# A post-norm attention and feed-forward layer: output a step later, another order on VectorE, projection ahead of x's turn

## The chip, the cores and the metric

One core of one Trainium2 chip runs the whole layer in one launch. The metric is the device time of an execution in microseconds (us). The three runs of the kernel before took 2051.58, 2055.7 and 2059.28 us, a median of 2055.7 us.

## What is computed

The input x has 8 sequences of 1024 tokens with 256 features, all f32. The layer is attention with ternary weights and then a feed-forward part with blockwise FP4 values, each followed by a residual sum and a layer norm:

```
x = _layernorm(x + attention(x))            # 16 heads of 16
gate = fp4_linear(x, w_gate)                # 256 -> 704
y = fp4_linear(x, w_up)
h = jax.nn.silu(gate) * y
x = _layernorm(x + fp4_linear(h, w_down))   # 704 -> 256
```

fp4_linear rounds both of its inputs in blocks of 16 to the grid 0, 0.5, 1, 1.5, 2, 3, 4, 6 times a scale of the block (its largest magnitude / 6), and multiplies in f32.

## The kernel before

Every engine has one program, and semaphores order them. `project` makes q, k and v, `attend` the attention, and `feed` the rest: output projection, first norm, FP4 rounding of x, gate and up, silu, FP4 rounding of h, down product, second norm, output. Only `feed` is changed. Its work is cut into 64 tiles of 128 tokens and runs as a software pipeline that is written out step by step: in step i each engine works on tile i - lag, and the order of its stages within the step is the order of the code. The first steps lie within the attention; from about 1470 us on nothing else runs.

The stages, with their engine, lag and lines in the kernel before:

- TensorE, in this order: x1_by_width (lag 3), x's turn by a product with the identity (L1354), which waits for xq of GpSimd and for the first copies of hT of ScalarE, since both share a bank of PSUM; output_projection (lag 1, L1286); down (lag 6, L1337, and L1345 for the last 64 rows of two tiles together, in every second step); gate_and_up (lag 3, L1298: 18 products); h_by_width (lag 5, h's turn, L1309).
- ScalarE: copy_xqT (L1446); output (lag 8: the shift L1375 and L1376, then L1384 into fin); bend_x (L1416, L1420); bend_h (L1426, L1430); silu (L1399); copy_hT (L1407, L1408, L1411); x1_normal (lag 1: L1375, L1376, L1392).
- VectorE: block maxima of h and x (L1482); xqT's low part (L1517); scales (L1466), reciprocals (L1472), divisions of x and h (L1488); y, the residual sum that reads the projection in PSUM (L1537); statistics of y (L1541, L1548); the add of xm (L1495, 256 columns) and the difference xg (L1552); z, the second residual sum (L1557); the add of hm (L1495, 704 columns); statistics of z (L1563, L1573); h (L1568), which reads up in PSUM.
- GpSimd: in the last ten tiles raw and xb (L1589, L1591); rstd of the first norm (L1579, L1580); xq (L1601); hg (L1608) and hq (L1613); rstd of the second norm (L1579, L1580 again).
- SyncE issues the loads of pairs of tiles and the store of a tile (L1259, lag 8).

The names `mv` and `rstd` hold mean, variance and the inverse deviation of the two norms, one column each; `z` and `fin` have two buffers by the tile's number, `x1` has seven. A wait `due(engine, name, t.lin(1, c))` asks that the stage that signals `name` has been done for tile t and c - 1 tiles more.

## Time and profile before

| | |
|---|---|
| median of 3 runs | 2055.7 us (2051.58 to 2059.28) |
| profiled execution | 2051.83 us, span 2050.0 us |
| TensorE busy | 1987.0 us, 97% |
| VectorE busy | 1881.0 us, 92% |
| ScalarE busy | 1674.6 us, 82% |
| GpSimd busy | 751.6 us, 37% |
| granted TensorE clock, mean | 0.997 |

The profile is of one execution. PE is TensorE, PEld its weight loads, DVE VectorE, ACT ScalarE, POOL GpSimd, SPq the queue of SyncE. In a table of stretches a stretch has its busy time and its number of instructions for each engine. In a timeline an instruction stands with start, length, engine, line, operation, output and inputs; in brackets is how long its engine had been idle before it, and what ended that. In the waits, a row says who waited for whom: us in total, how often, the longest.

### The profile page before, as it was taken

What the parts mean: (1) busy time and instruction counts of PE and PEld (TensorE: products, weight loads), DVE (VectorE), ACT (ScalarE), POOL (GpSimd) and SP (SyncE); (2) the same over time, 40 slices, a digit from 0 to 9 for tenths busy, and PEclk for the clock granted to TensorE, in tenths of its full rate; (3) what the DMA queues carried; (4) which work ended last, traced back from release to release, by engine and by line L of the source; (5) the groups of instructions that cost most, each with busy time, mean ns of one, the idle gap of its engine ahead of it and who ended that gap; (6) DMA issues with size and microseconds to landing.
All of it is one profiled execution on the core that took longest, in us unless ns stands there. A gap on an engine that the chain in (4) does not pass through costs nothing.

```text
span 2050.0 us, 42089 instructions
## 1 busy us (share of the span) xinstructions
PE 1987.0 (97%) x15806; PEld 1044.0 (51%) x15806; DVE 1881.0 (92%) x2345; ACT 1674.6 (82%) x3244; POOL 751.6 (37%) x749
## 2 busy tenths in 40 slices
PE   8999999999999999999999999999999999999997
PEld 7766333333333333333333333334477777777775
DVE  4788999999999999999999999997399999999996
ACT  6656888888888888888889888888877777777775
POOL 3000446665764561100010010000155555555784
PEclk9999999999999999999999999999999999999999
DMA  7885632444354354435435444542111111111210
GB/s 234 273 248 200 110 51 45 79 96 91 75 100 93 78 95 90 90 82 103 89 71 101 91 84 88 97 91 75 43 40 47 47 40 42 47 47 52 62 32 21
DMA packets 119000, 181.40 MB, mean 88 GB/s; under 512 B 29644, under 2 KB 74444, under 8 KB 118796
## 3 DMA queue, kind: packets, MB, share of 16 engines
q1 hardware_dynamic: 111116, 171.10, 36.2%
q10 hardware_dynamic: 7392, 7.34, 1.1%
q8 instruction: 125, 2.05, 0.5%
q14 instruction: 79, 0.65, 0.1%
q0 software_dynamic: 288, 0.27, 0.1%
HBM read 103.68 MB, written 73.40 MB: 86 GB/s over the span
## 4 chain that ended last, share of the span: by engine, by line
PE 68%; POOL 13%; issue 7%; ACT 7%; DVE 4%; DMA 1%; POOLq 0%; SPq 0%; DVEq 0%
PE ps L913 29%; PE ps L966 28%; POOL hq L1613 4%; PE ps L494 4%; POOL hg L1608 4%; POOL rstd L1580 3%; PE ps L504 3%; ACT craw L1033 2%; PE ps L935 2%; POOL fq L1601 2%; POOL rstd L1579 1%; ACT xm L1420 1%; ACT bend_of_x L1416 1%; PE ps L481 1%; ACT centre L1376 1%
## 5 line engine op out<-in xcount | busy, mean ns | idle before, releaser
L1079 DVE TENSOR_REDUCE negmax<-ps 128x1 f32<-128x1024 f32 x980 | 1182.5, 1219 | 19.7 <-PE ps L913 14.1
L1025 ACT ACTIVATE room<-ps 128x512 f32<-128x512 f32 x2048 | 1102.8, 599 | 118.3 <-PE ps L935 86.7
L935 PE MATMUL ps<-qs,ks 50*128 50x512 f32 x2048 | 745.6, 449 | 1.9 <-ACT room L1025 1.0
L913 PE MATMUL ps<-ks,qs 48*128 48x512 f32 x1960 | 714.5, 444 | 0.0
L966 PE MATMUL ps<-room,vals 128*17 128x256 f32 x8192 | 637.3, 385 | 8.9 <-ACT craw L1033 0.2
L913 PEld LDWEIGHTS ps<-ks,qs 48*128 48x128 f32 x1960 | 288.6, 184 | 414.3 <-DVE negmax L1079 333.0
L164 POOL CAST mrow<-turned_rows 128x32 fp32r<-128x32 f32 x32 | 6.7, 210 | 904.3 <-DVE turned_rows L159 690.8
L966 PEld LDWEIGHTS ps<-room,vals 128*17 128x17 f32 x8192 | 140.0, 95 | 371.4 <-issue 209.5
L935 PEld LDWEIGHTS ps<-qs,ks 50*128 50x128 f32 x2048 | 304.2, 184 | 18.2 <-ACT room L1025 14.3
L1298 PE MATMUL ps<-wguT,xqT 128*128 128x512 f32 (+1 forms) x1152 | 266.8, 384 | 1.4 <-DVE xqT L1517 1.4
L1298 PEld LDWEIGHTS ps<-wguT,xqT 128*128 128x128 f32 x1152 | 210.8, 188 | 48.9 <-issue 9.6
L1337 PE MATMUL ps<-wdT,hT 128*128 128x256 f32 x640 | 150.6, 382 | 5.0 <-ACT hT L1408 5.0
L1136 POOL TENSOR_SCALAR fq<-fq 88x1024 f32<-88x1024 f32 (+1 forms) x42 | 137.5, 3274 | 3.6
L1375 ACT ACTIVATE centre<-mv 128x1 f32<-128x1 f32 x128 | 25.5, 199 | 132.5 <-POOL rstd L1580 132.3
L1337 PEld LDWEIGHTS ps<-wdT,hT 128*128 128x128 f32 x640 | 122.1, 192 | 22.8 <-issue 5.6
L1608 POOL TENSOR_TENSOR hg<-room,hm 128x704 f32<-128x704 f32 x64 | 97.7, 1526 | 45.7 <-DVE room L1495 45.7
L1579 POOL TENSOR_TENSOR rstd<-mv,numbers 128x1 f32<-128x1 f32 x128 | 33.9, 265 | 202.1 <-DVE mv L1548 195.2
L1495 DVE TENSOR_TENSOR room<-room,hm 128x704 f32<-128x704 f32 x64 | 75.6, 1181 | 22.2 <-ACT hm L1430 21.8
L569 ACT ACTIVATE qf<-ps,b_col,s_all 128x512 f32<-128x512 f32 x64 | 49.9, 780 | 52.9 <-PE ps L494 50.0
L1613 POOL TENSOR_TENSOR hq<-hg,blocks 128x704 f32<-128x704 f32 x64 | 88.8, 1388 | 5.0
L494 PE MATMUL ps<-qs,wqk 128*128 128x512 f32 x256 | 80.4, 436 | 0.0
L1138 POOL TENSOR_TENSOR fq<-fq 88x1024 f32<-88x1024 f32 (+1 forms) x36 | 77.3, 2148 | 2.6
(111 smaller groups left out, 2154.3 us busy)
## 6 DMA issues: line engine op xcount, KB each, us to landing
qk_parts<-parts SPq DMA_DIRECT2D x64, 512.0 KB, 3.9
qs<-qk_parts SPq DMA_DIRECT2D x192, 128.0 KB, 4.5
ks<-qk_parts SPq DMA_DIRECT2D x192, 128.0 KB, 7.1
ctx_raw<-craw SPq DMA_DIRECT2D x64, 256.0 KB
ready<-passing SPq DMA_DIRECT2D x27, 512.0 KB, 6.6
pairs<-ready SPq DMA_DIRECT2D x27, 512.0 KB
out_dram<-fin SPq DMA_DIRECT2D x64, 128.0 KB, 1.7
xin<-in_L_attn_x_dram ACTq DMA_DIRECT2D x14, 512.0 KB, 5.5
```

The lines of the kernel that those rows point to most:

```text
L494: last = nc.tensor.matmul(ps[:, QK + m % 2, :], wqk[:, a, m // 2, c, (m % 2) * P:(m % 2 + 1) * P], x_half[:, i.slot(2), c, :], start=n == ...
L913: return nc.tensor.matmul(ps[:, MX + 2 * (item[i.k, u] % 2) + bank, :], qs[rows, i.slot(RING), pair, t * P:(t + 1) * P], ks[rows, i.slot(R ...
L935: nc.tensor.matmul(ps[:, score_bank(i, s, n), :], ks[rows, slot, pair, kt * P:(kt + 1) * P], qs[rows, slot, pair, qh * BANK:(qh + 1) * BAN ...
L966: last = nc.tensor.matmul(ps[h * AV:h * AV + DV, PV, cols], vals[:, i.k // NG * KT + kt, i.k % NG * GH + h, :], prob[:, prob_slot(i, s), h ...
L1025: nc.scalar.activation(prob[:, prob_slot(i, s), score_order(i, s)[n], :], ps[:, score_bank(i, s, n), :], ACT.Exp, scale=float(D) ** -0.5). ...
L1079: nc.vector.tensor_reduce(negmax[:, j.slot(RING), max_column(u):max_column(u) + 1], ps[:, bank:bank + 2, :], AX.XY, ALU.max, negate=True). ...
L1136: link(nc.gpsimd.tensor_scalar(dst, norm, mid * mid, gain, ALU.is_gt, ALU.mult))
L1138: link(nc.gpsimd.tensor_tensor(mag, mag, tmp, ALU.add))
L1298: last = nc.tensor.matmul(ps[:, GU + n0 // BANK, 0:n1 - n0], xqT[:, a, c, :], wguT[:, b, c, n0:n1], start=n == 0 and c == 0, stop=n == len ...
L1337: last = nc.tensor.matmul(ps[:, DN[t.slot(2)], 0:H], hT[:, c, :], wdT[:, c, :], start=c == 4, stop=False)
L1608: nc.gpsimd.tensor_tensor(hg[:, :], hn[:, t.slot(2)], hm[:, t.slot(2)], ALU.subtract).then_inc(sems["hgrid_ready"], 1)
L1613: nc.gpsimd.tensor_tensor(hq[:, :].rearrange("p (n e) -> p n e", e=BLK), hg[:, :].rearrange("p (n e) -> p n e", e=BLK), hs[:, t.slot(2), 1 ...
```

## The change

All of it is in `feed`. mv and rstd get a third column, so that the second norm has one column for even and one for odd tiles (`second(t)`); output and store of a tile come at lag 9 instead of 8, and there is one more step at the end. On TensorE the projection goes ahead of x's turn. On ScalarE x1_normal goes ahead of copy_hT. On VectorE y comes ahead of xqT's low part, the statistics of y together behind the divisions, and z with its statistics ahead of the add of hm. The last statistics of z (bn_aggr) wait for the output of the tile before last instead of the last one.

```diff
--- before.py
+++ after.py
@@ -52,7 +52,7 @@
 BQ = 32
 ARRIVED = 16 * 2 * (P // BQ)
 FILL = 3
-TILES_RUN = NTILES + 8
+TILES_RUN = NTILES + 9
 EPS = 1e-5
 STEP = 2.0 ** 22
 BEND = (STEP / 6.0) ** 0.5
@@ -1151,8 +1151,9 @@
     IC = (I + P - 1) // P
     NBX, NBH = H // BLK, I // BLK
     stats = sb("stats", [P, 2, 6])
-    mv = sb("mv", [P, 2, 2])
-    rstd = sb("rstd", [P, 2, 2])
+
+    mv = sb("mv", [P, 3, 2])
+    rstd = sb("rstd", [P, 3, 2])
     centre = sb("centre", [P, 2, 2])
     bend_of_x = sb("bend_of_x", [P, H])
     bend_of_h = sb("bend_of_h", [P, I])
@@ -1219,6 +1220,9 @@
     stored = [sem(f"stored{j}") for j in range(2)]
 
 
+    second = lambda t: 1 + t.slot(2)
+
+
     x_across = ps[:, HT + 1, H:2 * H]
 
     def due(eng, name, n):
@@ -1253,7 +1257,7 @@
             t = i.plus(2 * (PAIRS - 1))
             if i.k % 2 == 0 and i.k > 0 and t.ok(NT):
                 load(t)
-            t = i.plus(-8)
+            t = i.plus(-9)
             if t.ok(NT):
                 due(sp, "fin_ready", t.lin(1, 1))
                 sp.dma_start(out_tok[bass.ds(t.lin(P), P), :], fin[:, t.slot(2)]
@@ -1356,37 +1360,35 @@
             last.then_inc(sems["xt_psum"], 1)
 
         for i in each(ks):
-            order = ((3, x1_by_width), (1, output_projection), (6, down), (3, gate_and_up), (5, h_by_width))
             if i.k == FILL:
 
                 pe.wait_ge(wt_split, 2 * HC)
-                order = (order[1], order[0]) + order[2:]
-            for lag, stage in order:
+            for lag, stage in ((1, output_projection), (3, x1_by_width), (6, down), (3, gate_and_up), (5, h_by_width)):
                 if lag == 6 and 0 <= i.k - FILL < IC // 2:
                     wd_across(i.k - FILL)
                 if i.plus(-lag).ok(NT):
                     stage(i.plus(-lag))
 
-    def scalar(act, ks, lags=range(9)):
-        def shift(t, n, chain):
+    def scalar(act, ks, lags=range(10)):
+        def shift(t, n, at, chain):
 
 
             link = Chain(act, sems[chain], 2, t)
-            link(nc.scalar.activation(centre[:, n, 0:1], mv[:, n, 0:1], ACT.Copy, scale=-1.0))
-            link(nc.scalar.activation(centre[:, n, 1:2], centre[:, n, 0:1], ACT.Copy, scale=rstd[:, n, 1:2]))
+            link(nc.scalar.activation(centre[:, n, 0:1], mv[:, at, 0:1], ACT.Copy, scale=-1.0))
+            link(nc.scalar.activation(centre[:, n, 1:2], centre[:, n, 0:1], ACT.Copy, scale=rstd[:, at, 1:2]))
             link.close()
 
         def output(t):
             due(act, "rstd2_ready", t.lin(1, 1))
-            shift(t, 1, "shift2_chain")
+            shift(t, 1, second(t), "shift2_chain")
 
             wait(act, stored[t.slot(2)], t.turn(2, 16))
             nc.scalar.activation(fin[:, t.slot(2)], z[:, t.slot(2)], ACT.Identity, bias=centre[:, 1, 1:2],
-                                 scale=rstd[:, 1, 1:2]).then_inc(sems["fin_ready"], 1)
+                                 scale=rstd[:, second(t), 1:2]).then_inc(sems["fin_ready"], 1)
 
         def x1_normal(t):
             due(act, "rstd1_ready", t.lin(1, 1))
-            shift(t, 0, "shift1_chain")
+            shift(t, 0, 0, "shift1_chain")
 
             due(act, "z_used", t.lin(1, 1 - U))
             nc.scalar.activation(x1[:, t.slot(U)], y[:, :], ACT.Identity, bias=centre[:, 0, 1:2],
@@ -1447,8 +1449,8 @@
                                  ACT.Copy).then_inc(sems["xqT_high"], 1)
 
         for i in each(ks):
-            for lag, stage in ((3, copy_xqT), (8, output), (2, bend_x), (4, bend_h), (3, silu), (5, copy_hT),
-                               (1, x1_normal)):
+            for lag, stage in ((3, copy_xqT), (9, output), (2, bend_x), (4, bend_h), (3, silu), (1, x1_normal),
+                               (5, copy_hT)):
                 if lag in lags and i.plus(-lag).ok(NT):
                     stage(i.plus(-lag))
                 if lag == 3 and stage is copy_xqT and 0 <= i.k - FILL < IC // 2:
@@ -1512,6 +1514,17 @@
 
                 due(dve, "xq_ready", t2.lin(1, -1))
                 gx.top()
+            if on1:
+                due(dve, "wo_psum", t1.lin(1, 1))
+                pair, half = t1.k // 2, t1.k % 2
+                if t1.k < RAW:
+                    dve.wait_ge(pair_in[pair % PAIRS], pair_loads(pair))
+                else:
+                    dve.wait_ge(sems["xb_ready"], t1.k - RAW + 1)
+                due(dve, "x1_ready", t1.lin(1))
+                nc.vector.scalar_tensor_tensor(out=y[:, :], in0=ps[:, WO, 0:H], scalar=s_all[:, 3:4],
+                                               in1=pairs[:, pair % PAIRS, 1, half], op0=ALU.mult,
+                                               op1=ALU.add).then_inc(sems["wo_used"], 1)
             if on3:
                 due(dve, "xqT_high", t3.lin(1, 1))
                 nc.vector.tensor_tensor(xqT[:, 1].rearrange("p c n -> p (c n)"), x_across,
@@ -1527,26 +1540,14 @@
             if on4:
                 gh.divide().then_inc(sems["hn_ready"], 1)
             if on1:
-                due(dve, "wo_psum", t1.lin(1, 1))
-                pair, half = t1.k // 2, t1.k % 2
-                if t1.k < RAW:
-                    dve.wait_ge(pair_in[pair % PAIRS], pair_loads(pair))
-                else:
-                    dve.wait_ge(sems["xb_ready"], t1.k - RAW + 1)
-                due(dve, "x1_ready", t1.lin(1))
-                nc.vector.scalar_tensor_tensor(out=y[:, :], in0=ps[:, WO, 0:H], scalar=s_all[:, 3:4],
-                                               in1=pairs[:, pair % PAIRS, 1, half], op0=ALU.mult,
-                                               op1=ALU.add).then_inc(sems["wo_used"], 1)
                 due(dve, "wo_used", t1.lin(1, 1))
                 nc.vector.bn_stats(stats[:, 0], y[:, :]).then_inc(sems["stats1_ready"], 1)
-            if on2:
-                gx.add("xm_ready").then_inc(sems["xsum_ready"], 1)
-            if on1:
 
                 due(dve, "stats1_ready", t1.lin(1, 1))
                 due(dve, "rstd1_ready", t1.lin(1))
                 nc.vector.bn_aggr(mv[:, 0], stats[:, 0]).then_inc(sems["mv1_ready"], 1)
             if on2:
+                gx.add("xm_ready").then_inc(sems["xsum_ready"], 1)
                 due(dve, "xsum_ready", t2.lin(1, 1))
                 due(dve, "xq_ready", t2.lin(1))
                 nc.vector.tensor_tensor(xg[:, :], xn[:, :], xm[:, :],
@@ -1556,11 +1557,10 @@
                 due(dve, "fin_ready", t7.lin(1, -1))
                 nc.vector.tensor_tensor(z[:, t7.slot(2)], ps[:, DN[t7.slot(2)], 0:H], x1[:, t7.slot(U)],
                                         ALU.add).then_inc(sems["z_used"], 1)
+                due(dve, "z_used", t7.lin(1, 1))
+                nc.vector.bn_stats(stats[:, 1], z[:, t7.slot(2)]).then_inc(sems["stats2_ready"], 1)
             if on4:
                 gh.add("hm_ready").then_inc(sems["hsum_ready"], 1)
-            if on7:
-                due(dve, "z_used", t7.lin(1, 1))
-                nc.vector.bn_stats(stats[:, 1], z[:, t7.slot(2)]).then_inc(sems["stats2_ready"], 1)
             if on3:
                 due(dve, "silu_ready", t3.lin(1, 1))
                 due(dve, "up_psum", t3.lin(1, 1))
@@ -1569,8 +1569,8 @@
             if on7:
 
                 due(dve, "stats2_ready", t7.lin(1, 1))
-                due(dve, "fin_ready", t7.lin(1))
-                nc.vector.bn_aggr(mv[:, 1], stats[:, 1]).then_inc(sems["mv2_ready"], 1)
+                due(dve, "fin_ready", t7.lin(1, -1))
+                nc.vector.bn_aggr(mv[:, second(t7)], stats[:, 1]).then_inc(sems["mv2_ready"], 1)
 
     def gpsimd(pool, ks):
         def power(t, n, chain, name):
@@ -1617,8 +1617,8 @@
             t = i.plus(-7)
             if t.ok(NT):
                 due(pool, "mv2_ready", t.lin(1, 1))
-                due(pool, "fin_ready", t.lin(1))
-                power(t, 1, "pow2_chain", "rstd2_ready")
+                due(pool, "fin_ready", t.lin(1, -1))
+                power(t, second(t), "pow2_chain", "rstd2_ready")
 
     return Programs(sync, gpsimd, tensor, scalar, vector)
```

On TensorE, two steps in the middle of the feed-forward stretch. Before:

```order
L1309 MATMUL ps<-ident,hq 128x128 x6
L1354 MATMUL ps<-ident,fq 128x128 x2
L1286 MATMUL ps<-wT,pairs 128x256 x2
L1337 MATMUL ps<-wdT,hT 128x256 x5
L1345 MATMUL ps<-wdT,hT 128x256 x2
L1298 MATMUL ps<-wguT,xqT 128x512 x12
```

And now, L1313 being h's turn, L1290 the projection and L1358 x's turn:

```order
L1313 MATMUL ps<-ident,hq 128x128 x6
L1290 MATMUL ps<-wT,pairs 128x256 x2
L1358 MATMUL ps<-ident,fq 128x128 x2
L1341 MATMUL ps<-wdT,hT 128x256 x5
L1349 MATMUL ps<-wdT,hT 128x256 x2
L1302 MATMUL ps<-wguT,xqT 128x512 x12
```

The projection (L1286, now L1290) has changed places with x's turn (L1354, now L1358); nothing else moved on TensorE.

On ScalarE, from the bend of h to the next copy of xqT. Before, with L1399 silu, L1407 to L1411 the copies of hT and L1392 x1:

```order
L1426 ACTIVATE bend_of_h<-room 128x704
L1430 ACTIVATE hm<-bend_of_h,numbers 128x704
L1399 ACTIVATE room<-ps 128x704
L1407 ACTIVATE hT<-ps 128x128
L1408 ACTIVATE hT<-ps 64x128
L1411 ACTIVATE hT<-ps 128x512
L1375 ACTIVATE centre<-mv 128x1
L1376 ACTIVATE centre<-centre,rstd 128x1
L1392 ACTIVATE fq<-fq,centre,rstd 128x256
L1446 ACTIVATE xqT<-ps 128x256
```

And now:

```order
L1428 ACTIVATE bend_of_h<-room 128x704
L1432 ACTIVATE hm<-bend_of_h,numbers 128x704
L1401 ACTIVATE room<-ps 128x704
L1377 ACTIVATE centre<-mv 128x1
L1378 ACTIVATE centre<-centre,rstd 128x1
L1394 ACTIVATE fq<-fq,centre,rstd 128x256
L1409 ACTIVATE hT<-ps 128x128
L1410 ACTIVATE hT<-ps 64x128
L1413 ACTIVATE hT<-ps 128x512
L1448 ACTIVATE xqT<-ps 128x256
```

The shift and normalization of x1 (L1377, L1378, L1394) stand between silu and the copies of hT (L1409 to L1413). The output stands behind the copy of xqT in both, for a tile that is one older now.

On VectorE, from xqT's low part (L1517) to the add of hm (L1495, 128x704). Before:

```order
L1517 TENSOR_TENSOR xqT<-ps,xqT 128x256
L1466 SCALAR_TENSOR_TENSOR blocks<-blocks,numbers 128x60
L1472 RECIPROCAL blocks<-blocks 128x60
L1488 SCALAR_TENSOR_TENSOR fq<-fq,blocks 128x256
L1488 SCALAR_TENSOR_TENSOR room<-room,blocks 128x704
L1537 SCALAR_TENSOR_TENSOR fq<-ps,s_all,pairs 128x256
L1541 BN_STATS stats<-fq 128x6
L1495 TENSOR_TENSOR fq<-fq,xm 128x256
L1548 BN_AGGR mv<-stats 128x2
L1552 TENSOR_TENSOR fq<-fq,xm 128x256
L1557 TENSOR_TENSOR room<-ps,fq 128x256
L1495 TENSOR_TENSOR room<-room,hm 128x704
```

And now, beginning one row earlier, behind the block maxima:

```order
L1525 SCALAR_TENSOR_TENSOR fq<-ps,s_all,pairs 128x256
L1530 TENSOR_TENSOR xqT<-ps,xqT 128x256
L1468 SCALAR_TENSOR_TENSOR blocks<-blocks,numbers 128x60
L1474 RECIPROCAL blocks<-blocks 128x60
L1490 SCALAR_TENSOR_TENSOR fq<-fq,blocks 128x256
L1490 SCALAR_TENSOR_TENSOR room<-room,blocks 128x704
L1544 BN_STATS stats<-fq 128x6
L1548 BN_AGGR mv<-stats 128x2
L1497 TENSOR_TENSOR fq<-fq,xm 128x256
L1553 TENSOR_TENSOR fq<-fq,xm 128x256
L1558 TENSOR_TENSOR room<-ps,fq 128x256
L1561 BN_STATS stats<-room 128x6
```

y (L1537, now L1525) moved ahead of xqT's low part, both statistics of y stand together, and z with its statistics (L1558, L1561) ahead of the add of hm, which is the next row.

## Rows read from the trace of the kernel before

**Rows 1.** The page's first part: busy us, share of the span, instructions
```profile
PE 1987.0 (97%) x15806; PEld 1044.0 (51%) x15806; DVE 1881.0 (92%) x2345; ACT 1674.6 (82%) x3244; POOL 751.6 (37%) x749
```

**Rows 2.** Table of stretches: PE, PEld, DVE, ACT, POOL busy (instructions), PEclk, DMA share, GB/s
```profile
1500.00:2000.00 500.00, 475.48 (x2385) 391.97 (x2385) 468.83 (x966) 363.75 (x848) 316.15 (x416) 1.00 0.15 46
1900.00:2000.00 100.00, 95.18 (x478) 78.23 (x477) 96.61 (x195) 73.81 (x171) 83.42 (x99) 1.00 0.16 48
2000.00:2025.00 25.00, 23.63 (x123) 19.66 (x122) 20.84 (x42) 17.15 (x41) 14.09 (x18) 1.00 0.05 16
```

**Rows 3.** Groups of TensorE, 1500 to 2000 us: busy, mean ns, idle before, releasers
```profile
L1354 PE MATMUL ps<-ident,fq 128*128 128x128 f32 x112 | 23.1, 288 | 24.5 <-ACT hT L1408 20.1 <-POOL fq L1601 4.4
```

**Rows 4.** Waits, 1500 to 2000 us
```profile
POOL rstd L1579 <- DVE mv L1548: 134.2, 57, 3.2
ACT centre L1375 <- POOL rstd L1580: 113.8, 56, 2.2
```

**Rows 5.** Timeline of TensorE, two steps
```profile
1763.08 0.41 PE L1354 MATMUL ps<-ident,fq 128*128 128x128 f32 x2 [0.76 <-ACT hT L1408]
1763.33 1.03 PE L1286 MATMUL ps<-wT,pairs 128*128 128x256 f32 x4
1764.19 2.32 PE L1337 MATMUL ps<-wdT,hT 128*128 128x256 f32 x10
...
1767.08 4.13 PE L1298 MATMUL ps<-wguT,xqT 128*128 128x512 f32 x18
1771.05 0.82 PE L1309 MATMUL ps<-ident,hq 128*128 128x128 f32 x6
1772.04 0.41 PE L1354 MATMUL ps<-ident,fq 128*128 128x128 f32 x2 [0.18 <-ACT hT L1408]
```

**Rows 6.** Timeline of the other engines, the same steps
```profile
1761.29 0.55 POOL L1580 TENSOR_TENSOR rstd<-rstd,numbers 128x1 f32<-128x1 f32 x1
...
1761.75 0.74 ACT L1399 ACTIVATE room<-ps 128x704 f32<-128x704 f32 x1
1761.81 0.62 POOL L1601 TENSOR_TENSOR fq<-fq,blocks 128x256 f32<-128x256 f32 x1
1761.88 1.30 DVE L1495 TENSOR_TENSOR room<-room,hm 128x704 f32<-128x704 f32 x1 [0.38 <-ACT hm L1430]
...
1762.67 0.27 ACT L1408 ACTIVATE hT<-ps 64x128 f32<-64x128 f32 x1
...
1763.26 1.53 POOL L1608 TENSOR_TENSOR hg<-room,hm 128x704 f32<-128x704 f32 x1 [0.83 <-DVE room L1495]
...
1764.86 1.39 POOL L1613 TENSOR_TENSOR hq<-hg,blocks 128x704 f32<-128x704 f32 x1
...
1766.48 0.55 POOL L1580 TENSOR_TENSOR rstd<-rstd,numbers 128x1 f32<-128x1 f32 x1
1766.92 0.42 DVE L1488 SCALAR_TENSOR_TENSOR fq<-fq,blocks 128x256 f32<-128x256 f32 x1
1767.06 0.20 ACT L1375 ACTIVATE centre<-mv 128x1 f32<-128x1 f32 x1 [2.18 <-POOL rstd L1580]
...
1768.13 0.40 ACT L1416 ACTIVATE bend_of_x<-fq 128x256 f32<-128x256 f32 x1
...
1769.71 0.34 POOL L1579 TENSOR_TENSOR rstd<-mv,numbers 128x1 f32<-128x1 f32 x1 [2.68 <-DVE mv L1548]
...
1769.92 0.42 DVE L1557 TENSOR_TENSOR room<-ps,fq 128x256 f32<-128x256 f32 x1
...
1770.71 1.30 DVE L1495 TENSOR_TENSOR room<-room,hm 128x704 f32<-128x704 f32 x1 [0.38 <-ACT hm L1430]
```

**Rows 7.** Instructions by line: L1495 and L1466, shortest, median and longest ns
```profile
L1495 DVE TENSOR_TENSOR room<-room,hm x64: 881/1300/1373, 1481.6 to 2032.5; 128x704 f32<-128x704 f32 x64
L1466 DVE SCALAR_TENSOR_TENSOR blocks<-blocks,numbers x66: 166/529/1216, 1448.3 to 2028.0; 128x60 f32<-128x60 f32 x62, 128x16 f32<-128x16 f32 x2, 128x44 f32<-128x44 f32 x2
```

**Rows 8.** Waits, 2025 to 2050 us
```profile
ACT centre L1375 <- POOL rstd L1580: 11.7, 4, 4.0
```

## The prediction

> **What bounds the kernel now.** I read the page first. TensorE is busy 97% of the span, VectorE 92%, so some engine is nearly full all the time [rows 1]; the question is who is full in the stretch that the change touches. The feed-forward steps run from about 1470 us to the end. The table of stretches cuts out 1500 to 2000 us: TensorE 475.48 us busy, VectorE 468.83 us in 966 instructions [rows 2]. A step has 17 VectorE instructions, so the stretch holds 966 / 17 = 56.8 steps of 500 / 56.8 = 8.80 us, with 8.37 us of TensorE work in each. In the timeline the same instruction returns after 1770.71 - 1761.88 = 8.83 us [rows 6].
>
> The groups then say where TensorE's missing 24.5 us (500 - 475.5) went: all of it stands before one group, the turn of x (L1354), 20.1 us until ScalarE's copy L1408, 4.4 us until GpSimd's L1601 [rows 3]. TensorE stops at one point of a step and nowhere else.
>
> Why does it stop there? The waits name a ring: ScalarE waited 113.8 us for rstd from GpSimd (L1580), GpSimd 134.2 us for VectorE's statistics (L1548) [rows 4], VectorE 0.38 us a step for ScalarE's hm [rows 6]. The timeline shows one round of it, and the reader is to follow the ends into the starts [rows 6]: GpSimd finishes the second norm's rstd at 1766.48 + 0.55 = 1767.03; ScalarE, which stood idle 2.18 us for it, computes shift and output, 1.07 us from start to start, and only then x's bend at 1768.13, although its input was there at 1766.92 + 0.42 = 1767.34 (L1488), some 0.76 us earlier with the usual gap of 0.03. VectorE's adds and statistics hang on that bend; GpSimd starts rstd of the first norm at 1769.71, after 2.68 us of idle time, then xq (L1601, the round before at 1761.81). VectorE's add of hm (L1495) at 1770.71 had waited for hm behind the same ScalarE queue; it lasts 1.30 us where its fastest took 0.88 [rows 7], and GpSimd's L1608 waits 0.83 us for it. L1608, the product L1613 behind it and rstd close the round. So the output of a finished tile, which nobody needs, sits in the middle of the ring. TensorE's stop is fed by it: ScalarE is late with silu (1761.75) and so with the copies L1407 and L1408, and L1354 starts 0.76 us late in one step, 0.18 us in the next [rows 5, 6].
>
> **The change part by part.**
>
> *Output a step later.* No instruction is added: 128 shifts, 64 outputs and 64 stores stay. ScalarE now finds rstd of the tile in the buffer, so the 2.18 us wait goes, x's bend can start when xn is there, 0.76 us earlier, and hm with it. The 0.38 us that VectorE waits for hm goes. What the lag puts in its place: z's second buffer is free only after the output of two tiles ago, now in the same step as z's write. Even today's output, which waits for rstd, is through by 1768.2, and z's write (L1557) comes at 1769.92 [rows 6]: 1.7 us of cover, and more once the output no longer waits. The store moves one step back on SP's queue, behind at most one load of a pair; fin has two buffers and a store two steps to land. I cost both at nothing. The extra step at the end holds one output only.
>
> *Projection before x's turn on TensorE.* Its two products (four records) take 0.86 us from 1763.33 to 1764.19 [rows 5]. They need nothing that is late. Put first, they cover 0.86 us of the wait for the copies, more than the 0.76 and the 0.18. On its own this would move nothing, since the ring through the output sets 8.83 us and TensorE would wait elsewhere; with the ring cut it is worth all of the stop.
>
> *x1's normalization before the copies of hT on ScalarE.* This speaks against the change: shift and normalization are of the shapes of shift and output, 1.07 us from start to start [rows 6], put ahead of the copies that TensorE waits for. Laid out from gate-and-up's start: gate's product is ready after 12 of 18 products, some 2.65 us; silu (0.74) ends at 3.5; x1 to 4.6; the two small copies (0.27 each) at 5.1. TensorE ends gate-and-up at 1771.05 - 1767.08 = 3.97 and the turn of h at 4.78, the projection at 5.64 [rows 5, 6]. So 0.5 us is left, if rstd of the first norm is there when silu ends. It was there 0.65 us before (1761.84 against 1762.49), and VectorE's new order makes it earlier.
>
> *VectorE's order.* The read of the projection in PSUM moves up before xqT's low part; statistics and their sum stand right behind the divisions; z, its statistics and then the add of hm. TensorE waits for xqT's low part before gate-and-up; it is about 0.40 us later, with the down products between x's turn and gate-and-up, 2.9 us in the step shown (1764.19 to 1767.08) [rows 5], as cover. VectorE's own sum: 468.8 / 56.8 = 8.25 us a step, less the stretched 0.42 of L1495 and about 0.3 of L1466 (0.53 in the middle, 0.17 at least) [rows 2, 7], plus 0.15 for pairs that now follow each other with a wait on the result, is 7.7 us. What is left of stretching (the trace shows neither this order nor its meetings) is between 0 and 0.75, the whole of today's. I take 0.3, since the largest op now starts behind z, near L1601. 8.0 us stays under TensorE's 8.37.
>
> Stretching is plain in the rows: L1495 lasts 0.88 to 1.37 us for one shape [rows 7], and 1.30 where L1601 began 0.07 us before it [rows 6]. The Trainium skill (SBUF — State Buffer, "Who interferes with whom") says that a VectorE instruction with two SBUF inputs and a GpSimd instruction that reads SBUF exclude each other, the second blocked until the first has finished. The trace agrees in the pair just named: 1762.43, L1601's end, plus 0.88 is 1763.31, and L1495 ended at 1763.18.
>
> *Sum.* If TensorE becomes the bound, a step takes 8.37 us. Of the 24.5 us I leave 1.4 us in the ten last steps, in which GpSimd also makes raw and xb and its L1601 is what TensorE waits for, and 1.6 us for seams of a full TensorE that idle time hides today: 21.5 us. Between 2000 and 2025 us TensorE idles 25.0 - 23.63 = 1.4 us [rows 2]: 0.5. Before 1500 us nothing, since no output is in the ring there. In the tail ScalarE waits 11.7 us for rstd in four waits [rows 8], with the bend of h, the last copies of hT and the next output queued behind. That a wait goes shortens the tail only by what stood ready behind it, between 0 and 11.7 us; I take the output's own 1.07 us in three of the four places, 3 us. Together 25 us. The profiled execution took 2051.83 us (span 2050.0), so 2026.8; the median of the runs is 2055.7, and 25 us below it is 2030.7. **2031 us.** About 0.5% (10 us) is what a measurement of this kernel can tell from no change.
>
> **The rivals.**
>
> *TensorE is the bound, as summed:* 2031, with 2024 to 2037 as its own range (floor 8.3 to 8.45 us, tail 0 to 4). For it: the stop stands at one place and both its feeders move off. Chance 0.68.
>
> *The ring through VectorE and GpSimd still sets the step.* A division or add meets one of GpSimd's long products (1.53 and 1.39 us [rows 6]), so that xq or hq come late: 8.6 us a step instead of 8.8, 0.2 x 57 = 11 us, and 2 of the tail: 2042. For it: VectorE at 8.0 has only 0.37 us of room. Against it: the steps from 1900 us on carry raw and xb on GpSimd as well and last 100 / (195 / 17) = 8.72 us today [rows 2], so more on GpSimd does not by itself lengthen a step. Chance 0.14. The Trainium skill's rule (same page and section), taken for the whole length of every such instruction, would make a floor of its own: GpSimd 2 x (0.34 + 0.55) + 0.62 + 1.53 + 1.39 = 5.3, VectorE's six with two SBUF inputs 2 x 0.88 + 3 x 0.42 + 0.2 = 3.2, together 8.5 us, which gives 0.13 x 57 = 7 us less gain, 2038; it is part of this rival's chance. With raw and xb it would ask for some 9.7 us, and the 8.72 there contradict that.
>
> *TensorE was never full.* The ends of its products are modelled; if they give, the step falls to VectorE's 8.1 us: 0.7 x 57 = 40 us, 2016. Against it: gate-and-up's 18 records start 0.22 us apart over 3.97 us without a gap [rows 5]. Chance 0.05.
>
> *The stop only moves.* The copies of hT, now behind x1's normalization, or xqT's low part, are late by what the projection covers: 0.43 us a step again, only the tail gains: 2051, no change. Chance 0.08.
>
> *Slower.* rstd of the first norm comes later than 0.5 us after silu's end. Then ScalarE stands in x1's shift with the copies behind it, TensorE waits for them, and its next products, gate-and-up and thus the next silu, follow late. At 1 us too late the stop is 0.5 to 0.8 us in place of 0.43, and each step gains up to 0.35 us: 57 x 0.35 = 20 less 3: 2073. It decides at 0.5 us, against today's 0.65 us early. Chance 0.05.
>
> **How the numbers follow.** Faster by over 0.5% (under 2045): 0.68 + 0.14 + 0.05 = 0.87; same 0.08; slower 0.05. The range runs from 2022, the better end of the likeliest case with a little of the case below it, to 2045, which takes in the rival at 2042 and the spread of the runs (3.6 us to either side). It leaves out the two dear cases and most of the cheap one.
>
> **What would show it.** Right: in the middle of the stretch steps of 8.4 us, no idle time before x's turn, VectorE and ScalarE waiting for TensorE (products of gate and up), ScalarE's wait for rstd gone, L1495's counterpart near 1.0 us. Wrong: idle time before x's turn or gate-and-up with the copies, xqT or xq as releaser; steps of 8.6 with VectorE at full and stretched adds; ScalarE waiting for the first rstd.

## The result and the profile after

The changed kernel took 2022.62 us (median of 4 runs, 2016.67 to 2024.02), the kernel before 2053.64 us in the same round; the ratio is 0.984, 95% interval 0.981 to 0.987. A second round gave 0.984 again (0.981 to 0.987). So it is 31 us faster where 25 were forecast, and the median lies 0.6 us above the lower end of the range.

| | before | after |
|---|---|---|
| profiled execution, span | 2051.83, 2050.0 us | 2024.02, 2022.2 us |
| first read of the projection (y) on VectorE, from the start | 1440.1 us | 1448.1 us |
| from there to the end (the stretch, below) | 609.9 us | 574.1 us |
| first y to first h | 35.3 | 34.0 |
| first h to last h, 63 steps | 550.8 | 519.8 |
| last h to the end | 23.9 | 20.4 |
| middle step (11th to 51st h, / 40) | 8.83 | 8.21 |

Two rows stand for the steps: first and last start of the 64 products h on VectorE (the two times before the semicolon), in the kernel before and in the change:

```profile
L1568 DVE TENSOR_TENSOR room<-room,ps x64: 861/864/887, 1475.3 to 2026.1; 128x704 f32<-128x704 f32 x64
```

```profile
L1568 DVE TENSOR_TENSOR room<-room,ps x64: 873/875/889, 1482.1 to 2001.9; 128x704 f32<-128x704 f32 x64
```

The stretch became 35.8 us shorter, the span only 27.8 us, because the profiled execution of the change reached its first y 8 us later. What runs up to there is `project` and `attend`, which the change doesn't touch. The table of stretches shows why (columns as in [rows 2]); first the kernel before, then the change:

```profile
200.00:225.00 25.00, 24.40 (x219) 9.07 (x217) 23.57 (x23) 21.84 (x42) 0.00 (x0) 1.00 0.89 157
1440.00:1475.00 35.00, 33.92 (x285) 16.07 (x284) 7.46 (x22) 30.11 (x63) 3.55 (x8) 0.95 0.12 44
```

```profile
200.00:225.00 25.00, 24.55 (x143) 9.08 (x142) 16.63 (x17) 15.48 (x29) 0.00 (x0) 0.66 0.89 159
1440.00:1475.00 35.00, 34.32 (x324) 14.81 (x324) 6.85 (x17) 33.18 (x69) 2.14 (x5) 1.00 0.09 33
```

From 200 to 225 us the granted clock of the change is 0.66: part of it at 1.2 instead of 2.4 GHz, a loss of 0.34 x 25 = 8.5 us. I put it down to the execution and not to the kernel: the code that runs there is the same, and runs of the kernel before with a mean granted clock of 0.998 took 2048.5 to 2050.9 us, those with 0.992 took 2057.6 to 2059.6. This is most of the spread of the runs, and it is why I compare the variants below by the stretch, in which they differ, and by the ratio of their times. One of the four runs of full_rows (below) took 2942.7 us at a mean granted clock of 0.557, and its ratio is taken from the other three.

The kernel before lost some clock within the stretch as well: 0.95 between 1440 and 1475 us is 1.7 us of it, and the table shows 1.3 us between the first y and the first h that no part of the change accounts for.

The first part of the page:

```profile
PE 1983.0 (98%) x15806; PEld 1039.8 (51%) x15806; DVE 1859.8 (92%) x2345; ACT 1680.1 (83%) x3244; POOL 753.0 (37%) x749
```

The groups of TensorE and the waits between 1500 and 1950 us, against [rows 3, 4]. Of the groups, the turn of x, first in the kernel before, then in the change; the waits are those of the change:

```profile
L1354 PE MATMUL ps<-ident,fq 128*128 128x128 f32 x102 | 20.9, 287 | 22.3 <-ACT hT L1408 19.7 <-POOL fq L1601 2.6
```

```profile
L1358 PE MATMUL ps<-ident,fq 128*128 128x128 f32 x108 | 21.3, 279 | 2.0 <-ACT hT L1410 1.9
```

```profile
POOL rstd L1579 <- DVE mv L1548: 93.9, 49, 2.6
ACT bend_of_x L1418 <- DVE fq L1490: 63.6, 55, 2.4
POOL hg L1608 <- DVE room L1497: 43.8, 53, 0.8
ACT room L1401 <- PE ps L1302: 15.1, 24, 0.6
DVE room L1568 <- PE ps L1302: 11.5, 24, 0.5
```

ScalarE's wait for rstd is gone; it now waits for VectorE's division, and ScalarE and VectorE wait for TensorE's products. TensorE's idle time before x's turn fell from 22.3 to 2.0 us. At the end of the stretch it still stops: 4.5 us between 1896 and 2002 us, in seven stops of up to 1.1 us, each of them for the second copy of hT. Five of the seven lie between 1895 and 1976 us, where GpSimd also makes raw and xb.

```profile
L1358 PE MATMUL ps<-ident,fq 128*128 128x128 f32 x24 | 4.8, 281 | 4.5 <-ACT hT L1410 4.5
```

The timeline of TensorE, against [rows 5], is without a gap:

```profile
1764.07 4.21 PE L1302 MATMUL ps<-wguT,xqT 128*128 128x512 f32 x18
1768.12 0.82 PE L1313 MATMUL ps<-ident,hq 128*128 128x128 f32 x6
1768.77 1.03 PE L1290 MATMUL ps<-wT,pairs 128*128 128x256 f32 x4
1769.66 0.41 PE L1358 MATMUL ps<-ident,fq 128*128 128x128 f32 x2
1769.91 2.32 PE L1341 MATMUL ps<-wdT,hT 128*128 128x256 f32 x10
1772.16 0.70 PE L1349 MATMUL ps<-wdT,hT 64*128 64x256 f32 x4
1772.80 4.12 PE L1302 MATMUL ps<-wguT,xqT 128*128 128x512 f32 x18
```

And the other engines in that step, with silu of the next, against [rows 6]:

```profile
1763.13 0.60 ACT L1386 ACTIVATE fin<-room,centre,rstd 128x256 f32<-128x256 f32 x1
...
1764.21 0.42 DVE L1490 SCALAR_TENSOR_TENSOR fq<-fq,blocks 128x256 f32<-128x256 f32 x1
...
1764.67 0.42 ACT L1418 ACTIVATE bend_of_x<-fq 128x256 f32<-128x256 f32 x1 [0.93 <-DVE fq L1490]
...
1767.14 0.62 POOL L1601 TENSOR_TENSOR fq<-fq,blocks 128x256 f32<-128x256 f32 x1
1767.26 0.76 ACT L1401 ACTIVATE room<-ps 128x704 f32<-128x704 f32 x1
1767.47 1.03 DVE L1497 TENSOR_TENSOR room<-room,hm 128x704 f32<-128x704 f32 x1
...
1769.25 0.27 ACT L1410 ACTIVATE hT<-ps 64x128 f32<-64x128 f32 x1
...
1775.90 0.76 ACT L1401 ACTIVATE room<-ps 128x704 f32<-128x704 f32 x1 [0.63 <-PE ps L1302]
```

x's bend follows its division (L1490) at once, and the output runs at 1763.13, before it. The add of hm (L1497) lasts 1.03 us instead of 1.30.

### The profile page after: what moved, and what is told of

Same layout as the page of the kernel before. It is cut to its first block, busy times and chain, and to the rows that moved or that the text cites. A ratio compares the mean times of both kernels' runs of the same rounds, so it can differ in the third digit from the quotient of the medians.

```text
span 2022.2 us, 42087 instructions
## 1 busy us (share of the span) xinstructions
PE 1983.0 (98%) x15806; PEld 1039.8 (51%) x15806; DVE 1859.8 (92%) x2345; ACT 1680.1 (83%) x3244; POOL 753.0 (37%) x749
## 4 chain that ended last, share of the span: by engine, by line
PE 88%; DVE 5%; ACT 3%; issue 2%; DMA 1%; POOL 0%; SPq 0%; DVEq 0%; POOLq 0%; ACTq 0%
PE ps L913 30%; PE ps L966 28%; PE ps L1302 10%; PE ps L1341 5%; PE ps L494 4%; PE ps L504 3%; PE ps L1290 2%; ACT craw L1033 2%; PE ps L935 2%; PE ps L1313 2%; PE ps L481 1%; PE ps L1349 1%; DVE room L1490 1%; PE ps L1358 1%; DVE room L1568 1%
## 5 line engine op out<-in xcount | busy, mean ns | idle before, releaser
L1302 PE MATMUL ps<-wguT,xqT 128*128 128x512 f32 (+1 forms) x1152 | 267.0, 385 | 3.9 <-DVE xqT L1530 3.9
L1302 PEld LDWEIGHTS ps<-wguT,xqT 128*128 128x128 f32 x1152 | 210.8, 188 | 51.6 <-issue 9.9
L1341 PEld LDWEIGHTS ps<-wdT,hT 128*128 128x128 f32 x640 | 115.2, 190 | 17.2 <-issue 2.4
L1418 ACT ACTIVATE bend_of_x<-fq 128x256 f32<-128x256 f32 x64 | 26.7, 418 | 75.4 <-DVE fq L1490 75.4
L1580 POOL TENSOR_TENSOR rstd<-rstd,numbers 128x1 f32<-128x1 f32 x128 | 82.7, 646 | 10.0
```

Source lines behind the costliest of these rows:

```text
L1302: last = nc.tensor.matmul(ps[:, GU + n0 // BANK, 0:n1 - n0], xqT[:, a, c, :], wguT[:, b, c, n0:n1], start=n == 0 and c == 0, stop=n == len ...
L1341: last = nc.tensor.matmul(ps[:, DN[t.slot(2)], 0:H], hT[:, c, :], wdT[:, c, :], start=c == 4, stop=False)
L1580: nc.gpsimd.tensor_tensor(rstd[:, n, 1:2], rstd[:, n, 0:1], numbers[:, 1:2], ALU.pow).then_inc(sems[name], 1)
```

## The experiments

Each variant was timed against the kernel before on the same chip, except where one run is named. Stretch and middle step are taken as in the table above, from one profiled execution of each; the tail is the time from the last h to the end. The ring theory is the prediction's: rstd, output, bends of x and h, the add of hm, GpSimd's products and the next rstd wait for each other in a circle, and one round of it is the step. A meeting is an instruction of VectorE and one of GpSimd that run at the same time, of which one then lasts longer.

| | middle step | stretch | ratio (95%) |
|---|---|---|---|
| before | 8.83 | 609.9 | |
| the change | 8.21 | 574.1 | 0.984 (0.981 to 0.987) |
| out_only | 8.61 | 592.8 | 0.992 (0.989 to 0.995) |
| projection_only | 8.82 | 607.8 | 0.999 (0.997 to 1.000) |
| vector_order_only | 8.61 | 598.0 | 0.996 (0.994 to 0.997) |
| out_and_projection | 8.18 | 572.4 | 0.982 (0.980 to 0.985) |
| change_again | 8.21 | 574.1 | 0.984 (0.981 to 0.987) |
| change_without_projection | 9.03 | 618.6 | 1.004 (1.003 to 1.005) |
| change_output_at_8 | 8.42 | 586.9 | 0.989 (0.986 to 0.991) |
| change_two_products | 8.04 | 564.5 | one run, 2008.8 us |
| change_copies_first | 8.18 | 573.3 | 0.985 (0.980 to 0.989) |
| change_vector_order_of_before | 8.20 | 573.9 | one run, 2019.6 us |
| before_two_products | 8.82 | 608.4 | one run, 2056.8 us |
| full_rows | 8.20 | 573.0 | 0.983 (0.980 to 0.986) |

**out_only.** This is the kernel before with the parts of the diff that carry `second(t)` and the lags 8 to 9, and nothing else (cut here to the lags):

```diff
-            t = i.plus(-8)
+            t = i.plus(-9)
...
-            for lag, stage in ((3, copy_xqT), (8, output), (2, bend_x), (4, bend_h), (3, silu), (5, copy_hT),
+            for lag, stage in ((3, copy_xqT), (9, output), (2, bend_x), (4, bend_h), (3, silu), (5, copy_hT),
```

> The kernel before with output, store and doubled factors at lag 9 alone; the orders of TensorE, ScalarE and VectorE stay. Ring theory: the output leaves the ring, but TensorE still waits for the copies of hT, so the step falls from 8.83 to about 8.55 us and the feed-forward stretch (first read of the projection to the end, 609.9 us before, 574.1 after) to about 591; ratio near 0.991. Rival (the meetings of VectorE and GpSimd are what costs): the step stays above 8.7, stretch above 600, ratio 0.995 or more.

Measured 8.61 us and 592.8 us. That is half of the stretch's gain, 3.2 us of it in the tail, but only 0.22 of the 0.62 us of the middle step. TensorE still stops before x's turn, 8.5 us between 1600 and 1900 us. The stretching of the add of hm is gone as well, with VectorE's order as it was; fastest, median and slowest ns:

```profile
L1499 DVE TENSOR_TENSOR room<-room,hm x64: 878/881/894, 1483.2 to 2021.1; 128x704 f32<-128x704 f32 x64
```

The scales last 0.21 us in the mean instead of 0.54. So this run took the output out of the ring and most of the stretching with it, and it can't tell the rival (the meetings) from the ring theory: the rival's 8.7 us supposed that the meetings would stay. change_output_at_8, below, parts the two better.

**projection_only.** This is the kernel before with the projection ahead of x's turn.

```diff
-            order = ((3, x1_by_width), (1, output_projection), (6, down), (3, gate_and_up), (5, h_by_width))
...
-            for lag, stage in order:
+            for lag, stage in ((1, output_projection), (3, x1_by_width), (6, down), (3, gate_and_up), (5, h_by_width)):
```

> Only the projection ahead of x's turn. Ring theory: nothing, step 8.83 us, stretch 610, ratio 1.000, and TensorE's idle time moves to another place in the step. Rival (TensorE's own stop is worth its 0.43 us wherever the ring stands): step 8.4, ratio 0.988.

Measured 8.82 us, ratio 0.999. Between 1600 and 1900 us a part of the stop has moved to gate and up, where TensorE and its weight loads wait for xqT's low part, 6.6 us; 5.7 us are left before x's turn, where the kernel before had 16.0 us:

```profile
L1354 PE MATMUL ps<-ident,fq 128*128 128x128 f32 x68 | 13.9, 286 | 5.7 <-ACT hT L1406 5.1 <-POOL fq L1599 0.5
L1298 PE MATMUL ps<-wguT,xqT 128*128 128x512 f32 (+1 forms) x615 | 141.1, 382 | 6.6 <-DVE xqT L1515 6.6
PEld ps L1298 <- DVE xqT L1515: 18.4, 32, 0.8
```

**out_and_projection.** This run has both of the above.

> Output at lag 9 and the projection ahead of x's turn; ScalarE's and VectorE's orders stay as before. Ring theory: this is the whole gain, TensorE full, step 8.20 us, stretch 574, ratio 0.984 like the change. Rival (VectorE's order is needed for the last part): step 8.35 to 8.5, stretch 583 or more, ratio above 0.988.

```profile
L1570 DVE TENSOR_TENSOR room<-room,ps x64: 867/870/889, 1478.2 to 1995.8; 128x704 f32<-128x704 f32 x64
```

Measured 8.18 us and 572.4 us, with 517.6 us from the first to the last h (the row above): all of the gain, and 1.7 us of stretch more than the change gained. VectorE's and ScalarE's new orders are not needed.

**vector_order_only.** This is the kernel before with VectorE's order of the change (the cut leaves out that the statistics of y now stand together ahead of the add of xm).

```diff
+            if on1:
+                due(dve, "wo_psum", t1.lin(1, 1))
...
-            if on4:
-                gh.add("hm_ready").then_inc(sems["hsum_ready"], 1)
-            if on7:
                 due(dve, "z_used", t7.lin(1, 1))
                 nc.vector.bn_stats(stats[:, 1], z[:, t7.slot(2)]).then_inc(sems["stats2_ready"], 1)
+            if on4:
+                gh.add("hm_ready").then_inc(sems["hsum_ready"], 1)
```

> Only VectorE's order (y early, both statistics pairs together, z ahead of the add of hm). Ring theory: rstd of the first norm and xq come earlier in the ring, so it shortens, step 8.5 to 8.65 us, stretch 597 to 601, ratio near 0.994. Rival (the order only evades stretching, 0.42 us at most of it on the ring): with stretching gone and the ring as it is, step 8.4, stretch 586. Rival (no effect, the output holds the ring): 610.

Measured 8.61 us, 598.0 us. On its own this order shortens the step by 0.22 us. The reason that I expected, that rstd of the first norm and xq are made earlier in the ring, is not shown apart from the other one, that it evades stretching. The add of hm is still stretched in part, but the scales are no longer (0.21 us in the mean between 1600 and 1900 us, 0.54 in the kernel before):

```profile
L1495 DVE TENSOR_TENSOR room<-room,hm x64: 890/1033/1254, 1483.3 to 2023.2; 128x704 f32<-128x704 f32 x64
L1466 DVE SCALAR_TENSOR_TENSOR blocks<-blocks,numbers 128x60 f32<-128x60 f32 x35 | 7.3, 209 | 0.0
```

The rival's step of 8.4 us was not reached.

**change_vector_order_of_before.** This is the change with VectorE's old order.

> The change with VectorE's order of before (only its factors doubled). Theory: TensorE is full either way, VectorE's order is worth nothing on top, step 8.20 to 8.22 us, stretch 573 to 576. Rival (VectorE's order is needed): step 8.3 or more, stretch over 578.

Measured 8.20 us, 573.9 us (one execution): with the ring cut elsewhere, the order is worth nothing.

**change_again.** This is the change itself.

> The change once more, beside the next three. Ring theory: TensorE full in the middle, step 8.21 us, feed-forward stretch 574 us, ratio 0.984. Rival (the size of the gain was a chance of one chip): step or ratio off by more than 0.1 us or 0.004.

Measured 8.21 us, 574.1 us, ratio 0.984.

**change_without_projection.** This is the change with TensorE's order of before.

> The change with TensorE's order of before (x's turn first), all else kept. ScalarE's copies of hT now stand behind x1's normalization and nothing covers them. Ring theory: TensorE stops again before x's turn for the copies, 0.45 us a step or more; step 8.65 to 8.75, stretch 598 to 602, ratio 0.993, worse than out_only (592.8). Rival (the projection's place is worth only what it is in the kernel before, nothing): step 8.2, stretch 575.

Measured 9.03 us, 618.6 us: dearer than I expected and slower than before, by 0.3 to 0.5%. Its timeline shows the new ring (L1302 gate and up, L1403 silu, L1379 and L1396 x1, L1313 h's turn, L1412 the second copy, L1358 x's turn):

```profile
1701.14 4.13 PE L1302 MATMUL ps<-wguT,xqT 128*128 128x512 f32 x18
...
1704.25 0.76 ACT L1403 ACTIVATE room<-ps 128x704 f32<-128x704 f32 x1 [1.24 <-PE ps L1302]
...
1704.91 0.19 ACT L1379 ACTIVATE centre<-mv 128x1 f32<-128x1 f32 x1
...
1705.11 0.81 PE L1313 MATMUL ps<-ident,hq 128*128 128x128 f32 x6
...
1705.46 0.60 ACT L1396 ACTIVATE fq<-fq,centre,rstd 128x256 f32<-128x256 f32 x1
...
1706.13 0.26 ACT L1412 ACTIVATE hT<-ps 64x128 f32<-64x128 f32 x1
...
1706.53 0.41 PE L1358 MATMUL ps<-ident,fq 128*128 128x128 f32 x2 [0.60 <-ACT hT L1412]
```

silu starts 3.11 us after gate and up, x1's shift and normalization go first, and TensorE waits 0.60 us for the second copy with h's turn done. Against out_only (8.61 us) this run has two other orders, ScalarE's and VectorE's. VectorE's made the kernel before faster, and the timeline points to ScalarE's, but no run has TensorE's old order with ScalarE's alone.

**change_copies_first.** This is the change with `(5, copy_hT), (1, x1_normal)` in ScalarE's old order.

> The change with ScalarE's order of before: copies of hT ahead of x1's normalization. In the change the second copy ends 0.1 us before TensorE has finished the projection, so this order of ScalarE is a risk that the change takes without a gain. Theory: TensorE is as full as before, step 8.18 instead of 8.21 us, stretch 572 to 575. Rival (the normalization ahead of the copies brings part of the gain): step 8.25 or more, stretch 577 or more.

Measured 8.18 us, 573.3 us: the middle step gains 0.03 us and all steps 2.0 us, of which the tail gives 1.2 us back (21.6 us after the last h instead of 20.4). That may not be the order's doing: in this one execution a scale of the tail met GpSimd's product and lasted 1.37 us instead of 0.54, and the granted clock was 0.72 from 2001 to 2007 us.

**change_output_at_8.** This is the change with output and store back at lag 8.

> The change with output and store back at lag 8, in the step in which rstd is made; all orders of the change kept. Ring theory: ScalarE waits for rstd again, with x's bend behind it, but VectorE's order leaves the ring near TensorE's sum: step 8.35 to 8.45, stretch 586 to 590, ratio 0.989; the tail is as long as before (24 us instead of 20.4). Rival (output's lag is the whole gain): step 8.7 or more, stretch over 600.

Measured 8.42 us, 586.9 us, tail 22.8 us where I expected 24. Here the output alone costs 0.21 us a step, and not by stretching: the add of hm lasts 0.89 us in the median against 1.03 in the change. The tail follows the output's lag in both directions, 20.4 and 20.7 us with lag 9 (the change and out_only), 22.8 and 23.9 with lag 8 (this run and the kernel before). In the kernel before the granted clock was 0.66 from 2032 to 2037 us of the tail; the product that it lengthened had ended by 2036.87, before ScalarE's wait for rstd ended at 2037.31, so little of the difference can be the clock's.

**change_two_products** and **before_two_products.** Both leave out the product of x's low part with the weights' high part, each in one execution:

```diff
-                for n, (a, b) in enumerate(PRODUCTS):
+                for n, (a, b) in enumerate(PRODUCTS[:2]):
```

> The change with two instead of three of the products of gate and up (the low part of x times the high part of the weights is left out), 6 of 18 records or 1.3 us a step less on TensorE. Ring theory: TensorE was the bound, the next one (VectorE with GpSimd) stands just behind it: step 8.05 to 8.1, stretch about 568, and TensorE idle by more than 1 us a step. Rival (nothing but TensorE bounds): step 6.9 to 7.2. Rival (TensorE was not the bound of the change): step stays 8.2.

> The kernel before with two instead of three of the products of gate and up (low part of x times high part of the weights left out), 1.3 us a step less on TensorE. Ring theory: TensorE did not bound the kernel before, step 8.83 us as it was, stretch 605 to 610 (tail and start shorten a little). Rival (TensorE's work was on the path): step 7.5 to 8.4.

Measured 8.04 and 8.82 us. With 1.3 us less on TensorE the change gains only 0.17 us, the kernel before nothing: TensorE bounds the change, the ring bounded the kernel before, and the next bound lies right behind. It is VectorE, which is busy 293.6 of 300 us in change_two_products and waits for nobody (columns as in [rows 2]):

```profile
1600.00:1900.00 300.00, 263.79 (x1343) 211.79 (x1343) 293.63 (x632) 237.84 (x558) 199.59 (x265) 1.00 0.17 52
```

TensorE's idle time before x's turn, 1600 to 1900 us, first the change, then the kernel before:

```profile
L1358 PE MATMUL ps<-ident,fq 128*128 128x128 f32 x74 | 15.1, 286 | 36.2 <-ACT hT L1410 36.2
```

```profile
L1354 PE MATMUL ps<-ident,fq 128*128 128x128 f32 x68 | 14.7, 300 | 51.3 <-ACT hT L1408 48.8 <-POOL fq L1601 2.5
```

**full_rows.** This is an attempt at a better version, on out_and_projection (cut: wdT also gets one more column block, in which ScalarE writes the zeros):

```diff
-                nc.tensor.matmul(ps[:, DN[tile.slot(2)], 0:H], hT[rows, IC - 1, :], wdT[rows, IC - 1, :],
+                nc.tensor.matmul(ps[:, DN[tile.slot(2)], 0:H], hT[:, IC - 1, :], wdT[:, IC - 1 + tile.slot(2), :],
```

> out_and_projection, and the two products of hT's last 64 rows made as products over 128 rows, with weights that are zero in the other tile's rows. TensorE's weight loads stand still 0.33 us before and after the 64-row products, in every second step. If that is a cost of changing between 64 and 128 rows, the pair of steps loses 0.5 us, the step goes from 8.18 to 7.95 at most, and VectorE's and GpSimd's 8.04 (change_two_products) bounds it: 8.04 to 8.08, stretch 565 to 568, ratio 0.979. Rival (the stand is the wait for the product's own data): step 8.18, stretch 572.

Measured 8.20 us, 573.0 us: a miss. The timeline of TensorE:

```profile
1700.87 2.32 PE L1341 MATMUL ps<-wdT,hT 128*128 128x256 f32 x10
1703.03 1.03 PE L1349 MATMUL ps<-wdT,hT 128*128 128x256 f32 x4
1703.71 4.21 PE L1302 MATMUL ps<-wguT,xqT 128*128 128x512 f32 x18
```

The pair of products takes 0.68 us (1703.03 to 1703.71) where the 64-row pair takes 0.64 (1772.16 to 1772.80 above), and the down product ahead of it 2.16 instead of 2.25. Together that is 2.84 instead of 2.89 us. The stands of the weight loads vanish and nothing comes of it, so they had cost TensorE next to nothing. The fastest version stays out_and_projection, whose lead over the change is beyond what the runs can tell (ratios 0.982 and 0.984).

## Why the prediction came out as it did

- *The output sits in the ring.* Right. Taking it out alone brings 17 of the 36 us of stretch, the wait for rstd is gone from the waits, and putting it back into the change costs 12.8 us. How much of the 17 us is the output's 1.07 us in the ring and how much the add's 0.42 us of stretching, which went with it, stays open.
- *The projection alone moves nothing; with the ring cut it takes the stop.* Right: 0.999 alone, and 20.4 us of stretch on top of out_only.
- *VectorE's order as no part of the sum.* Right on top of the others, but the reason given ("8.0 us stays under TensorE's 8.37") was close: change_two_products puts that side at 8.04, TensorE at 8.18 to 8.21. Alone the order is worth 12 us of stretch. The 0.3 us kept for stretching was about right: the add of hm has 0.15 (1.03 against 0.88) and the scales (L1468) 0.13, with a mean of 0.34 us where out_only has 0.21 (1600 to 1900 us, the row below). The "0.17 at least" of L1466 in the prediction belongs to its smaller shapes. With VectorE's old order only the add's part is gone, and the scales last 0.37.

```profile
L1468 DVE SCALAR_TENSOR_TENSOR blocks<-blocks,numbers 128x60 f32<-128x60 f32 x36 | 12.2, 339 | 0.0
```

- *Tail 3 us.* It was 3.5.
- *Start: nothing.* It is 1.3 us less, but the variants with all three products have 33.9 or 34.0 us there, projection_only too, so it is not the change's; the 0.95 of granted clock from 1440 to 1475 us in the kernel before is a loss of about 1.7 us.
- *The floor of 8.37 us.* This is the step that failed: the term "475.48 us of TensorE work in 56.8 steps". With TensorE full the step is 8.21 us (8.18 in out_and_projection), so the floor was 0.16 us too high, 0.16 x 57 = 9 us of gain. Two smaller terms were off as well. "1.6 us for seams" was an allowance that no trace of the kernel before showed, and no such loss appears in the timeline of the change. "1.4 us in the ten last steps" was too little, since 4.5 us of stops stay from 1896 us on. From the first to the last h I forecast 21.5 + 0.5 = 22 us and 31.0 came; 9 + 1.6 - 3.1 is 7.5 of the 9 us between them. The mechanism was right, and the size of its largest term was not.

What the floor had wrong is how busy time was read. The records of products that follow each other overlap: gate and up at 1764.07 lasts 4.21 us, to 1768.28, and the next product starts at 1768.12. Where a gap follows, nothing overlaps the end of the last record, and this end is counted as busy. The turn of h is busy 0.82 us in both kernels, but where the projection follows at once it starts 0.65 us after it (1768.12 to 1768.77). The turn of h ahead of [rows 5] in the kernel before:

```profile
1761.51 0.82 PE L1309 MATMUL ps<-ident,hq 128*128 128x128 f32 x6
```

So the stop was not 0.76 and 0.18 us but 1763.08 - 1761.51 - 0.65 = 0.92 and 1772.04 - 1771.05 - 0.65 = 0.34, 0.63 us a step, and 8.83 - 0.63 = 8.20.

The medians, 31 us apart, show less of the gain than the stretch, and the forecast of 25 is 6 us off against them. That it is not further off is in part luck: the stops at the end cancel a third of the floor's error, and why the medians gained less than the stretch is shown only in part, by the 1.7 us of clock that the kernel before lost in it.

- *0.5 us left for the copies behind x1's normalization.* Wrong, though it cost little here. I let silu start 2.65 us after gate and up, with 12 of 18 products done; it starts 3.10 us after at best (1772.80 to 1775.90, where it waited for the product), and 3.19 in the step shown, behind hm (1764.07 to 1767.26). The second copy ends at 1769.52, x's turn could start at about 1769.63, and the margin is 0.1 us. From 1896 us on it is used up (the 4.5 us above), but out_and_projection, with ScalarE's old order, stops there as well, for 4.0 us. Without the projection the change is slower than the kernel before. The rival "slower" had its mechanism right; its trigger there is not rstd but the order itself, which the projection covers.
- *The Trainium skill's rule as a floor of 8.5 us.* The measured 8.04 us of change_two_products is below it. The exclusion of the Trainium skill (SBUF — State Buffer, "Who interferes with whom") shows in single pairs, but the durations of all GpSimd instructions and of all VectorE instructions with two inputs in SBUF do not add up to a floor.

## What to carry to other kernels

When engines wait in a ring, look for the instruction on it whose result nobody needs soon, and give it a step of lag and a second buffer; an order that shortens the ring elsewhere may then be worth nothing. Read what an engine can do at best from the starts of instructions that follow without a gap, not from busy time divided by steps, since the end of the record before each gap is counted as busy. And where an order puts work ahead of what the full engine waits for, test it without its cover: here the cover had 0.1 us to spare, and without it the step was 9.0 instead of 8.2 us.

## What the runs showed that I had not expected

The granted clock went to half for 7 to 17 us at the same place, 205 us after the start, in every profiled execution but those of the kernel before and of change_without_projection; TensorE had been busy 95.9 of 98 us there (102 to 200 us), in the kernel before as well. What tells the executions apart I can't say; no run was made for it. In the feed-forward stretch it stayed at 1.00 in the change, with TensorE full, while before_two_products, with TensorE idle 1.5 us a step, had 0.97 from 1500 to 2000 us (columns as in [rows 2]):

```profile
1500.00:2000.00 500.00, 417.01 (x2042) 340.07 (x2041) 471.33 (x966) 360.20 (x849) 313.51 (x413) 0.97 0.15 46
```

That GpSimd's rstd (L1580) is stretched in the change, 0.59 us in the median where it was 0.55, shows that meetings lengthen GpSimd's instructions too; it was off the path.
